# Self-attention in a transformer kernel: products of one or two units in 11 blocks, 11 key tiles summed by GpSimd, maxima negated in another form

## The chip, the cores and the metric

The kernel runs on one core of a Trainium2 chip. The metric is the time of one execution in device microseconds (us). Times inside the kernel are read from one profiled execution; its span starts at 0 and positions in it are given in us.

## The reference

Two transformer layers over x (2 x 2048 x 512), 16 heads of 32 channels each. The change lies in the only self-attention, that of the second layer, over all 2048 keys:

```python
scores = jnp.einsum('bqhd,bkhd->bhqk', qh, kh) / jnp.sqrt(jnp.asarray(d, q.dtype))
attn = jax.nn.softmax(scores, axis=-1)
out = jnp.einsum('bhqk,bkhd->bqhd', attn, vh)
```

Around it stand projections, a cross-attention over 77 context rows in each layer, normalizations and an MLP; they aren't touched.

## The kernel before

The function `attention` (L1592) works in 32 steps: 2 batches x 4 groups of 4 heads x 4 chunks of 512 queries. One step has 16 key tiles of 128 keys. Each engine has its own program with the same steps; semaphores join them. `run` (L1699) unrolls the first and last steps and loops over the rest.

**Two passes over the scores.** The softmax needs each query's largest score before the exponentials. So TensorE computes the scores twice. In the first form queries lie on the partitions: `score_unit` (L1785) is one matmul of 128 queries x 512 keys into one of three PSUM banks (`sm`), and VectorE's `peak_of_unit` (L1950) reduces it to its maxima. There are 64 units per step (4 heads x 4 query tiles x 4 key chunks). They run ahead: a step computes units 14 to 63 of the next step and 0 to 13 of the one behind that. A unit's matmul waits until the unit three before it has been reduced. When the last unit of a step is reduced (the 50th in the order of the running step, x = 49), `minus_peaks` (L1959) takes the maxima over the key chunks (`top`), negates them in two parts of lower precision (`neg_hi`, and the remainder) and lays them into `neg`; `turn_peaks` (L1801) transposes them on TensorE, ScalarE's `take_rows` (L1894) copies them out and a DMA spreads them into spare rows of `q`, so that the scores of the second pass come out with the maximum subtracted.

**The second pass.** `score_tile` (L1810): keys on the partitions, one matmul for each key tile and head, into one of three banks (`st`). ScalarE takes the exponential into `e` (`exponentials`, L1902), a ring of four tiles.

**The products.** `weigh` (L1822) multiplies a tile's exponentials by v for the four heads at once, each in its own 32 columns of the array, summed over the tiles in `acc[:, 0]`. `add_up` (L1837) does the same with a matrix of ones for the sums of the exponentials, in `acc[:, 1]`. To save such products, ten of the tiles (`POOLED`: 0, 1, 3, 4, 6, 7, 9, 10, 12, 13) are summed by GpSimd (`add`, L2021) into `esum`, which then needs one product. A unit of products is eight matmuls in the profile (four heads, each shown twice). A tile's place in the ring comes free when its products are done (`tile_used`) and, for a pooled tile, when GpSimd has added it (`e_added`).

**The order on TensorE** is written out in `step` (L1852). Behind each score matmul comes one unit of maxima. Behind the second head of every key tile comes a block of products (`weigh_tiles`): those of the tile before. A block has one unit for a pooled tile, two for another, three for the last, whose block holds `esum` as well: 16 blocks with 23 units.

```python
                        if NKT > 1 and h == 1:
                            if kt == 0 and exists(i, j - 1):
                                weigh_tiles(i, j - 1, [NKT - 1])
                            if kt > 0 and exists(i, j):
                                weigh_tiles(i, j, [kt - 1])
```

**The end of a step.** ScalarE copies `acc` to `sums` behind its exponentials of tile 0 of the next step (`fetch_sums`, L1921); only then may the next step's first product overwrite `acc`. VectorE transposes the sums of the exponentials, takes reciprocals, and transposes them back (`divide`, L1976) at the places `DIVIDE_AT` among its 64 reductions; GpSimd multiplies (`scale`, L2031) between its additions, and SyncE stores.

Of the kernel before, what the change touches and what calls it, by code (L numbers as in the profile page):

```python
# [7 lines left out]
F32 = mybir.dt.float32  # L8
F32R = mybir.dt.float32r
ALU = mybir.AluOpType  # L10
# [3 lines left out]
P = 128  # L14
B, T, C = 2, 2048, 512
S = 77
HEADS, DH = 16, 32
# [1574 lines left out]
def attention(nc, d, name, q_in, k_in, v_in, o_out, keys, preload):  # L1592
# [23 lines left out]

    POOLED = [t for t in range(NKT - 2) if t % 3 != 2] if NKT > 2 else []
    ADDS = max(len(POOLED) - 1, 0)
# [7 lines left out]
    LATE = 1 if NKT > 1 else 2  # L1626
    DIVIDE_AT = (6, 8, 32) if NKT > 1 else range(4)
    SETUP = 2 + KW % 2
    with nc.cleanup_on_exit(), ExitStack() as ctx:
# [15 lines left out]
        top = sb("top", [P, GH * TT])  # L1645
        neg_hi = sb("neg_hi", [P, GH * TT], F32R)
        neg = sb("neg", [P, TT, P])
        rows = sb("rows", [P, 2, W])
# [10 lines left out]
        unit_done, unit_read = sem("unit_done"), sem("unit_read")  # L1659
        top_done, neg_done, neg_ready = sem("top_done"), sem("neg_done"), sem("neg_ready")  # L1660
        score_done, score_read, tile_used, e_added = sem("score_done"), sem("score_read"), sem("tile_used"), sem("e_added")
# [6 lines left out]
        def exists(i, j):  # L1668

            return not isinstance(i, int) or 0 <= BODY * i + j < STEPS  # L1670
# [10 lines left out]
        def turned(i, j):  # L1681

            return number(i, j - 1, TURN) if j else 0
# [100 lines left out]
        def _(pe):  # L1784
# [16 lines left out]
            def turn_peaks(i, j):  # L1801

                pe.wait_ge(neg_ready, 2 * (BODY * i + j + 1))
                if j:
                    bank_free(pe, i, j - 1, TURN)
                for qt in range(TT):
                    mm = pe.transpose(st[:, TURN % RING if j else 0, qt * P:(qt + 1) * P], neg[:, qt], ident[:])
                mm.then_inc(score_done, 1)
# [28 lines left out]
            def add_up(i, j, kt):  # L1837

                if kt in POOLED:
                    return  # L1840
                first = min(t for t in range(NKT) if t not in POOLED)
                operands = [e[0:KR, (j * NKT + kt) % ER]]
                if POOLED and kt == NKT - 1:
                    pe.wait_ge(e_added, (BODY * i + j + 1) * ADDS)
                    operands.append(esum)
                for x, operand in enumerate(operands):
                    for h in range(GH):
                        mm = pe.matmul(acc[h * DH:(h + 1) * DH, 1], ones[0:KR], operand[:, h], start=(kt == first),  # L1848
                                       stop=(kt == NKT - 1 and x == len(operands) - 1), tile_position=(0, h * DH))
                mm.then_inc(tile_used, 1)  # L1850

            def step(i, j):  # L1852
                turn = exists(i, j + 1)
                units = units_of_step(i, j)
                given, scores = 0, 0
                if NKT == 1 and exists(i, j - 1):
                    weigh_tiles(i, j - 1, [0])
                for kt in range(NKT):
                    for h in range(GH):
                        if exists(i, j):  # L1860
                            score_tile(i, j, kt, h)
                        scores += 1
                        while given < len(units) and given * GH * NKT < scores * U:
                            score_unit(i, *units[given])
                            given += 1
                        if NKT > 1 and h == 1:
                            if kt == 0 and exists(i, j - 1):
                                weigh_tiles(i, j - 1, [NKT - 1])
                            if kt > 0 and exists(i, j):
                                weigh_tiles(i, j, [kt - 1])  # L1870
                    if kt == TURN_KT and turn:
                        turn_peaks(i, j + 1)
                for m, u in units[given:]:
                    score_unit(i, m, u)

            def weigh_tiles(i, j, tiles):

                for kt in tiles:
                    weigh(i, j, kt)
                    add_up(i, j, kt)  # L1880

# [11 lines left out]
        def _(act):  # L1893
# [33 lines left out]
            def step(i, j):  # L1927
                if NKT == 1 and exists(i, j - 1):
                    fetch_sums(i, j - 1)
                for kt in range(NKT):  # L1930
                    if exists(i, j):
                        exponentials(i, j, kt)
                    if NKT > 1 and kt == 4 and exists(i, j - 1):
                        spread_inverse(i, j - 1)
                    if NKT > 1 and kt == 0 and exists(i, j - 1):
                        fetch_sums(i, j - 1)
                    if kt == TURN_KT and exists(i, j + 1):
                        take_rows(i, j + 1)
# [10 lines left out]
        def _(dve):  # L1949
# [9 lines left out]
            def minus_peaks(i, j):  # L1959

                n = BODY * i + j
                dve.wait_ge(unit_read, (n + 1) * U + 2)
                if KC > 1:
                    dve.tensor_reduce(top[:], peak[:].rearrange("p (x c) -> p x c", c=KC), AX.X, ALU.max).then_inc(top_done, 1)
                    dve.wait_ge(top_done, n + 1)
                dve.tensor_scalar(neg_hi[:], top[:], -1.0, None, ALU.mult).then_inc(neg_done, 1)
                dve.wait_ge(neg_done, n + 1)
                if exists(i, j - 1):
                    dve.wait_ge(score_done, turned(i, j - 1) + 1)
                by_head = lambda ap: ap.rearrange("p (h t) -> p h t", t=TT)  # L1970
                parts = neg[:, :, 3 * DH:3 * DH + 2 * GH].rearrange("p t (h s) -> p h t s", s=2)
                dve.tensor_copy(parts[:, :, :, 0], by_head(neg_hi[:].bitcast(F32))).then_inc(neg_ready, 1)
                dve.scalar_tensor_tensor(out=parts[:, :, :, 1], in0=by_head(top[:]), scalar=-1.0, in1=by_head(neg_hi[:].bitcast(F32)),
                                         op0=ALU.mult, op1=ALU.subtract).then_inc(neg_ready, 1)
# [33 lines left out]
            dve.memset(ones[:], 1.0).then_inc(set_up, 1)  # L2008
            dve.memset(neg[:], 0.0).then_inc(set_up, 1)
            if KE > KW:  # L2010
# [9 lines left out]
        def _(pool):  # L2020
# [16 lines left out]
            def step(i, j):  # L2037
                if POOLED and exists(i, j):
                    for x in range(1, 6):
                        add(i, j, x)  # L2040
                if exists(i, j - LATE):
                    scale(i, j - LATE)
                if POOLED and exists(i, j):
                    for x in range(6, len(POOLED)):
                        add(i, j, x)
# [245 lines left out]
```

## Time and profile before

| | us |
|---|---|
| median of 3 runs | 4163.22 (4161.48 to 4164.41) |
| profiled execution | 4159.49 |
| its span | 4157.7 |
| TensorE busy, whole span | 3771.6 |
| VectorE | 2333.9 |
| ScalarE | 1867.3 |
| GpSimd | 2080.2 |
| self-attention, first unit to last copy of the sums | 905.6 to 2804.0 |

In the profile PE is TensorE's matmuls, PEld its weight loads (one in front of each matmul, and the place where it waits), DVE is VectorE, ACT ScalarE, POOL GpSimd. `a_` stands before the names of this function's tiles: `a_sm` and `a_st` are the scores of the two passes, `a_e` the exponentials, `a_peak` the maxima, `a_acc` the products. A row gives start, length, engine, line, operation, tiles and the count of instructions that it joins; in square brackets the idle time before it and what ended it. Lengths of matmuls are modelled; starts of weight loads are the better measure of TensorE's pace.

### The profile page before, as it was taken

How to read it: one execution, taken by the hardware profiler on the slowest of the kernel's cores; microseconds unless marked ns; L12 is line 12 of the kernel's file. 1: busy time of each engine (PE TensorE's matmuls, PEld its weight loads, DVE VectorE, ACT ScalarE, POOL GpSimd, SP SyncE). 2: the span in 40 equal slices, each digit the busy share in tenths (PEclk: the TensorE clock that was granted, in tenths of full speed). 3: DMA queues.
4: the chain of work that ended last, by engine and by line, in shares of the span. 5: the costliest groups of instructions: out<-in, count | busy, mean ns of one | idle time of the engine just before them, and what ended most of it. 6: DMA issues, size and time to landing. Idle time of an engine off the chain costs nothing. (4 is left out here: it accounts for less than half of the span.)

```text
span 4157.7 us, 58861 instructions
## 1 busy us (share of the span) xinstructions
PE 3771.6 (91%) x19596; PEld 2442.6 (59%) x19596; DVE 2333.9 (56%) x4020; ACT 1867.3 (45%) x3431; POOL 2080.2 (50%) x923
## 2 busy tenths in 40 slices
PE   4799969979999999999999999985999959999998
PEld 2577748854444444444444444433777737888887
DVE  2466642247777767776777777733676625222222
ACT  1465631115666656665666666663565521111111
POOL 0356630005778767776777777783676634000000
PEclk8788879978999999999999999997999869999999
DMA  7566657752130211203130211105567651211110
GB/s 230 133 158 173 168 154 220 227 137 62 26 67 16 64 27 38 46 23 67 26 67 15 65 26 26 31 18 134 135 165 173 164 166 56 81 40 40 40 40 30
DMA packets 213560, 371.98 MB, mean 89 GB/s; under 512 B 36103, under 2 KB 52999, under 8 KB 209703
## 3 DMA queue, kind: packets, MB, share of 16 engines
q1 hardware_dynamic: 213287, 368.49, 32.7%
q8 instruction: 153, 2.51, 0.3%
q14 instruction: 120, 0.98, 0.1%
HBM read 215.54 MB, written 144.51 MB: 87 GB/s over the span
## 5 line engine op out<-in xcount | busy, mean ns | idle before, releaser
L1957 DVE TENSOR_REDUCE a_peak<-a_sm 128x1 f32<-128x512 f32 x2048 | 1275.0, 682 | 470.5 <-PE a_sm L1797 464.5
L1911 ACT ACTIVATE a_e<-a_st 128x512 f32<-128x512 f32 x2048 | 1075.1, 600 | 718.2 <-PE a_st L1819 714.7
L2029 POOL TENSOR_TENSOR a_esum<-a_esum,a_e 128x2048 f32<-128x2048 f32 x256 | 1172.1, 4578 | 126.5 <-ACT a_e L1911 114.1
L1819 PE MATMUL a_st<-a_q,a_k 128*128 128x512 f32 x2048 | 870.2, 428 | 17.9 <-issue 12.9
L1797 PE MATMUL a_sm<-a_k,a_q 96*128 96x512 f32 x2048 | 831.8, 413 | 49.7 <-DMA a_k<-s_k 28.1
L1819 PEld LDWEIGHTS a_st<-a_q,a_k 128*128 128x128 f32 x2048 | 386.4, 189 | 536.7 <-ACT a_e L1911 269.9
L1832 PE MATMUL a_acc<-a_e,a_v 128*32 128x512 f32 x4096 | 547.2, 606 | 17.6 <-ACT a_sums L1925 16.7
L1797 PEld LDWEIGHTS a_sm<-a_k,a_q 96*128 96x128 f32 x2048 | 397.8, 194 | 148.8 <-DVE a_peak L1957 57.6
L2152 PE MATMUL mlp_ph<-mlp_us,mlp_w_hi 128*128 128x512 f32 x1024 | 336.3, 391 | 31.9 <-DVE mlp_raw_lo L2201 31.9
L2029 POOL TENSOR_TENSOR a_esum<-a_e 128x2048 f32<-128x2048 f32 x32 | 146.8, 4587 | 427.6 <-ACT a_e L1911 427.6
L2194 ACT ACTIVATE mlp_gelu<-mlp_ph,mlp_b 128x512 f32<-128x512 f32 x128 | 88.1, 688 | 595.4 <-PE mlp_ph L2152 595.4
L2209 DVE CAST mlp_gs<-mlp_gelu 128x512 fp32r<-128x512 f32 x128 | 91.4, 714 | 458.3 <-ACT mlp_gelu L2194 458.3
L2167 PE MATMUL mlp_py<-mlp_w_hi,mlp_gs 128*128 128x512 f32 x1024 | 317.7, 391 | 17.1 <-DVE mlp_gs L2211 17.1
L2232 POOL TENSOR_TENSOR mlp_x<-mlp_x,mlp_brow 128x2048 f32<-128x2048 f32 x8 | 37.0, 4626 | 569.5 <-DMA mlp_x<-s_x 569.3
L1409 POOL TENSOR_TENSOR p_e<-p_e,p_inv 128x308 f32<-128x308 f32 x256 | 173.4, 709 | 168.6 <-DVE p_inv L1093 168.6
L2152 PEld LDWEIGHTS mlp_ph<-mlp_us,mlp_w_hi 128*128 128x128 f32 x1024 | 193.2, 189 | 72.6 <-issue 32.3
L2167 PEld LDWEIGHTS mlp_py<-mlp_w_hi,mlp_gs 128*128 128x128 f32 x1024 | 192.0, 188 | 61.6 <-issue 16.5
L587 PE MATMUL p_sm<-p_ks,p_qs 96*128 96x78 f32 x1024 | 171.9, 310 | 47.7 <-DMA p_qs<-s_q 28.3
L587 PEld LDWEIGHTS p_sm<-p_ks,p_qs 96*128 96x128 f32 x1024 | 157.2, 222 | 80.9 <-issue 28.9
L1848 PE MATMUL a_acc<-a_e,a_ones 128*32 128x512 f32 x1536 | 201.4, 596 | 1.7 <-POOL a_esum L2029 1.7
L2167 PE MATMUL mlp_py<-mlp_raw_lo,mlp_gs 128*128 128x512 f32 x512 | 200.0, 391 | 0.0
L2152 PE MATMUL mlp_ph<-mlp_us,mlp_raw_lo 128*128 128x512 f32 x512 | 199.9, 390 | 0.0
(151 smaller groups left out, 5169.7 us busy)
## 6 DMA issues: line engine op xcount, KB each, us to landing
p_qs<-s_q SPq DMA_DIRECT2D x192, 256.0 KB, 5.7
s_q<-p_qo SPq DMA_DIRECT2D x64, 512.0 KB, 7.4
a_q<-s_q SPq DMA_DIRECT2D x96, 256.0 KB, 5.2
a_k<-s_k SPq DMA_DIRECT2D x24, 1024.0 KB, 15.5
s_x<-p_x SPq DMA_DIRECT2D x16, 1024.0 KB, 4.4
s_u<-p_ut_hi SPq DMA_DIRECT2D x64, 256.0 KB, 5.8
s_u<-p_ut_lo SPq DMA_DIRECT2D x64, 256.0 KB, 6.4
p_us<-s_u SPq DMA_DIRECT2D x16, 1024.0 KB, 7.8
```

The costliest lines, as they stand in the source:

```text
L587: mm = pe.matmul(sm[:, unit % 2, h * KE:(h + 1) * KE], qs[0:3 * DH, g % 2, h, qt * P:(qt + 1) * P], ks[0:3 * DH, b, g * GH + h], start=Tru ...
L1409: pool.tensor_tensor(e[:, number % 2, qt, :, 0:S], e[:, number % 2, qt, :, 0:S], inv[:, number % 2, qt].unsqueeze(2).to_broadcast([P, GH, ...
L1797: mm = pe.matmul(sm[:, bank_of_unit(j, u), x * KE:(x + 1) * KE], q[0:3 * DH, j % QR, h, qt * P:(qt + 1) * P], k[0:3 * DH, g % 2, h, kc * K ...
L1819: pe.matmul(st[0:KR, place(kt, h) % RING], k[:, g % 2, h, kt * P:kt * P + KR], q[:, j % QR, h], start=True, stop=True).then_inc(score_done, 1)
L1832: mm = pe.matmul(acc[rows, 0], v[0:KR, g % 2, kt, rows], e[0:KR, (j * NKT + kt) % ER, h], start=(kt == 0), stop=(kt == NKT - 1), tile_posi ...
L1848: mm = pe.matmul(acc[h * DH:(h + 1) * DH, 1], ones[0:KR], operand[:, h], start=(kt == first), stop=(kt == NKT - 1 and x == len(operands) - ...
L1911: act.activation(e[0:KR, (j * NKT + kt) % ER, h], st[0:KR, place(kt, h) % RING], ACT.Exp, scale=SCALE).then_inc(score_read, 1)
L1957: dve.tensor_reduce(dst, src, AX.X, ALU.max).then_inc(unit_read, 1)
L2029: pool.tensor_tensor(esum[:], e[:, slot(0)] if x == 1 else esum[:], e[:, slot(x)], ALU.add).then_inc(e_added, 1)
L2152: mm = pe.matmul(ph[:, m % 4], w1[pw][:, t, m * P:(m + 1) * P], us[:, b, pm, t], start=(t == 0 and s == 0), stop=(t == KT - 1 and s == 2))
L2167: mm = pe.matmul(py[:, tt], gs[:, m % 2, pw, tt * P:(tt + 1) * P], w2[pm][:, m], start=(m == 0 and s == 0), stop=(m == HT - 1 and s == 2))
L2209: dve.tensor_copy(gs[:, m % 2, 0], gelu[:, m % 2]).then_inc(g_hi, 1)
```

## The change

`POOLED` becomes 0, 1, 2, 4, 5, 7, 8, 10, 11, 12, 13: eleven tiles are summed by GpSimd in ten additions. A new function `products` writes the order of the blocks out: eleven blocks of two units, behind the second head of tiles 0, 1, 2, 4, 5, 7, 8, 10, 11, 13 and 15. The product of `esum` has a function of its own. The copy of `acc`, the places of the divisions and of GpSimd's scaling move to fit. `minus_peaks` has no tensor_scalar and no copy any more: two operations of two tensors and a scalar write the parts into `neg` directly, the first with a tensor of zeros.

```diff
-    POOLED = [t for t in range(NKT - 2) if t % 3 != 2] if NKT > 2 else []
+    POOLED = [0, 1, 2, 4, 5, 7, 8, 10, 11, 12, 13]
...
-    DIVIDE_AT = (6, 8, 32) if NKT > 1 else range(4)
+    DIVIDE_AT = (10, 12, 36)
...
-        neg_hi = sb("neg_hi", [P, GH * TT], F32R)
-        neg = sb("neg", [P, TT, P])
+        zeros = sb("zeros", [P, TT])
+        neg = sb("neg", [P, TT, P], F32R)
...
             def add_up(i, j, kt):
...
+                for h in range(GH):
+                    mm = pe.matmul(acc[h * DH:(h + 1) * DH, 1], ones[0:KR], e[0:KR, (j * NKT + kt) % ER, h], start=(kt == first),
+                                   stop=False, tile_position=(0, h * DH))
+                if kt < NKT - 1:
+                    mm.then_inc(tile_used, 1)
+
+            def add_partial(i, j):
+
+                pe.wait_ge(e_added, (BODY * i + j + 1) * ADDS)
+                for h in range(GH):
+                    mm = pe.matmul(acc[h * DH:(h + 1) * DH, 1], ones[0:KR], esum[:, h], start=False, stop=True, tile_position=(0, h * DH))
                 mm.then_inc(tile_used, 1)
+
+            def products(i, j, kt):
+
+                if kt == 0 and exists(i, j - 1):
+                    add_up(i, j - 1, 14)
+                    weigh(i, j - 1, 15)
+                elif kt == 1 and exists(i, j - 1):
+                    add_up(i, j - 1, 15)
+                    add_partial(i, j - 1)
+                elif kt == 2 and exists(i, j):
+                    weigh(i, j, 0)
+                    weigh(i, j, 1)
+                elif kt == 4 and exists(i, j):
+                    weigh(i, j, 2)
+                    weigh(i, j, 3)
+                elif kt == 5 and exists(i, j):
+                    add_up(i, j, 3)
+                    weigh(i, j, 4)
...
+                elif kt == 15 and exists(i, j):
+                    weigh(i, j, 13)
+                    weigh(i, j, 14)
...
-                        if NKT > 1 and h == 1:
-                            if kt == 0 and exists(i, j - 1):
-                                weigh_tiles(i, j - 1, [NKT - 1])
-                            if kt > 0 and exists(i, j):
-                                weigh_tiles(i, j, [kt - 1])
+                        if h == 1:
+                            products(i, j, kt)
...
-                    if NKT > 1 and kt == 0 and exists(i, j - 1):
+                    if kt == 1 and exists(i, j - 1):
                         fetch_sums(i, j - 1)
...
-                dve.tensor_scalar(neg_hi[:], top[:], -1.0, None, ALU.mult).then_inc(neg_done, 1)
-                dve.wait_ge(neg_done, n + 1)
...
-                dve.tensor_copy(parts[:, :, :, 0], by_head(neg_hi[:].bitcast(F32))).then_inc(neg_ready, 1)
-                dve.scalar_tensor_tensor(out=parts[:, :, :, 1], in0=by_head(top[:]), scalar=-1.0, in1=by_head(neg_hi[:].bitcast(F32)),
+                no_term = zeros[:].unsqueeze(1).to_broadcast([P, GH, TT])
+                dve.scalar_tensor_tensor(out=parts[:, :, :, 0], in0=by_head(top[:]), scalar=-1.0, in1=no_term, op0=ALU.mult,
+                                         op1=ALU.add).then_inc(neg_ready, 1)
+                dve.wait_ge(neg_ready, 2 * n + 1)
+                dve.scalar_tensor_tensor(out=parts[:, :, :, 1].bitcast(F32), in0=by_head(top[:]), scalar=-1.0, in1=parts[:, :, :, 0].bitcast(F32),
                                          op0=ALU.mult, op1=ALU.subtract).then_inc(neg_ready, 1)
...
                 if POOLED and exists(i, j):
-                    for x in range(1, 6):
+                    for x in range(1, 8):
                         add(i, j, x)
                 if exists(i, j - LATE):
                     scale(i, j - LATE)
                 if POOLED and exists(i, j):
-                    for x in range(6, len(POOLED)):
+                    for x in range(8, len(POOLED)):
                         add(i, j, x)
```

## Rows read from the trace of the kernel before

**Rows 1.** Busy time by engine in one step's length, with the granted clock.

```profile
2000.00:2057.40 57.40, 56.13 (x318) 27.58 (x317) 43.30 (x72) 35.30 (x68) 42.41 (x11) 1.00 0.10 24
```

The columns are: stretch, its length; busy us and instructions of PE, PEld, DVE, ACT, POOL; granted clock; share of the DMA engines; GB/s.

**Rows 2.** Instructions in order of time, ScalarE: copies of the sums.

```profile
1417.19 1.03 ACT L1925 ACTIVATE a_sums<-a_acc 128x1024 f32<-128x1024 f32 x1
...
1541.22 1.03 ACT L1925 ACTIVATE a_sums<-a_acc 128x1024 f32<-128x1024 f32 x1
...
1598.62 1.03 ACT L1925 ACTIVATE a_sums<-a_acc 128x1024 f32<-128x1024 f32 x1
```

**Rows 3.** In order of time, TensorE's weight loads around two ordinary blocks.

```profile
1506.09 0.19 PEld L1819 LDWEIGHTS a_st<-a_q,a_k 128*128 128x128 f32 x1 [0.84 <-ACT a_e L1911]
1506.20 0.19 PEld L1797 LDWEIGHTS a_sm<-a_k,a_q 96*128 96x128 f32 x1
...
1507.61 0.19 PEld L1797 LDWEIGHTS a_sm<-a_k,a_q 96*128 96x128 f32 x1
1508.15 0.16 PEld L1832 LDWEIGHTS a_acc<-a_e,a_v 128*32 128x32 f32 x8 [0.36 <-issue]
1509.15 0.19 PEld L1819 LDWEIGHTS a_st<-a_q,a_k 128*128 128x128 f32 x1 [0.84 <-ACT a_e L1911]
...
1511.22 0.16 PEld L1832 LDWEIGHTS a_acc<-a_e,a_v 128*32 128x32 f32 x8 [0.36 <-issue]
...
1513.08 0.19 PEld L1819 LDWEIGHTS a_st<-a_q,a_k 128*128 128x128 f32 x1 [0.84 <-issue]
```

**Rows 4.** The same view, the stretch in which the maxima are negated.

```profile
1523.13 0.19 PEld L1819 LDWEIGHTS a_st<-a_q,a_k 128*128 128x128 f32 x1 [0.84 <-issue]
...
1525.78 0.19 PEld L1797 LDWEIGHTS a_sm<-a_k,a_q 96*128 96x128 f32 x1 [1.17 <-DVE a_peak L1957]
1526.21 0.16 PEld L1832 LDWEIGHTS a_acc<-a_e,a_v 128*32 128x32 f32 x8 [0.24 <-issue]
```

**Rows 5.** In order of time, VectorE.

```profile
1506.86 1.89 DVE L1957 TENSOR_REDUCE a_peak<-a_sm 128x1 f32<-128x512 f32 x3 [0.58 <-PE a_sm L1797]
...
1519.98 2.48 DVE L1957 TENSOR_REDUCE a_peak<-a_sm 128x1 f32<-128x512 f32 x4 [0.58 <-PE a_sm L1797]
...
1522.75 1.75 DVE L1966 TENSOR_SCALAR a_neg_hi<-a_top 128x16 fp32r<-128x16 f32 x1
...
1525.03 2.49 DVE L1957 TENSOR_REDUCE a_peak<-a_sm 128x1 f32<-128x512 f32 x4
...
1544.14 0.69 DVE L1957 TENSOR_REDUCE a_peak<-a_sm 128x1 f32<-128x512 f32 x1 [1.17 <-PE a_sm L1797]
...
1546.70 1.82 DVE L1957 TENSOR_REDUCE a_peak<-a_sm 128x1 f32<-128x512 f32 x3
```

**Rows 6.** In order of time, GpSimd: two additions, the scaling, two additions.

```profile
1504.81 9.23 POOL L2029 TENSOR_TENSOR a_esum<-a_esum,a_e 128x2048 f32<-128x2048 f32 x2 [0.74 <-ACT a_e L1911]
1514.00 1.29 POOL L2035 TENSOR_TENSOR a_o<-a_sums,a_inv_t 128x512 f32<-128x512 f32 x1
1515.25 9.23 POOL L2029 TENSOR_TENSOR a_esum<-a_esum,a_e 128x2048 f32<-128x2048 f32 x2
```

**Rows 7.** VectorE beside GpSimd elsewhere; shortest/median/longest of such operations (ns).

```profile
150.23 1.27 POOL L1403 TENSOR_TENSOR p_us_lo<-p_us,p_us_hi 128x512 fp32r<-128x512 f32 x1
...
150.85 2.80 DVE L1161 SCALAR_TENSOR_TENSOR raw_p_lo<-raw_p,p_w 128x2048 fp32r<-128x2048 f32 x1
...
L1161 DVE SCALAR_TENSOR_TENSOR raw_p_lo<-raw_p,p_w x6: 2281/2288/2798, 96.5 to 3042.7; 128x2048 fp32r<-128x2048 f32 x6
...
3450.45 4.93 POOL L2225 TENSOR_TENSOR mlp_raw_lo<-mlp_raw,mlp_w_hi 128x2048 fp32r<-128x2048 f32 x1
3450.84 4.82 DVE L2209 CAST mlp_gs<-mlp_gelu 128x512 fp32r<-128x512 f32 x1
...
L2209 DVE CAST mlp_gs<-mlp_gelu x128: 418/427/4824, 3433.4 to 4142.3; 128x512 fp32r<-128x512 f32 x128
```

**Rows 8.** Weight loads in order of time: the first one behind a halt.

```profile
1475.77 0.29 PEld L1819 LDWEIGHTS a_st<-a_q,a_k 128*128 128x128 f32 x1 [6.88 <-issue]
```

More of the change, by code:

```diff
@@ L1626, in attention @@
     LATE = 1 if NKT > 1 else 2
-    DIVIDE_AT = (6, 8, 32) if NKT > 1 else range(4)
-    SETUP = 2 + KW % 2
+    DIVIDE_AT = (10, 12, 36)
+    SETUP = 3 + KW % 2
     with nc.cleanup_on_exit(), ExitStack() as ctx:
@@ L1659, in attention @@
         unit_done, unit_read = sem("unit_done"), sem("unit_read")
-        top_done, neg_done, neg_ready = sem("top_done"), sem("neg_done"), sem("neg_ready")
+        top_done, neg_ready = sem("top_done"), sem("neg_ready")
         score_done, score_read, tile_used, e_added = sem("score_done"), sem("score_read"), sem("tile_used"), sem("e_added")
@@ L1806, in turn_peaks @@
                 for qt in range(TT):
-                    mm = pe.transpose(st[:, TURN % RING if j else 0, qt * P:(qt + 1) * P], neg[:, qt], ident[:])
+                    mm = pe.transpose(st[:, TURN % RING if j else 0, qt * P:(qt + 1) * P], neg[:, qt].bitcast(F32), ident[:])
                 mm.then_inc(score_done, 1)
@@ L1837, in add_up @@
             def add_up(i, j, kt):
-                if kt in POOLED:
-                    return
                 first = min(t for t in range(NKT) if t not in POOLED)
[L1842 to L1849, printed above, removed]
@@ new lines, in products @@
+            def products(i, j, kt):
[14 more added lines that the diff above has]
+                    weigh(i, j, 4)
+                elif kt == 7 and exists(i, j):
+                    weigh(i, j, 5)
+                    weigh(i, j, 6)
+                elif kt == 8 and exists(i, j):
+                    add_up(i, j, 6)
+                    weigh(i, j, 7)
+                elif kt == 10 and exists(i, j):
+                    weigh(i, j, 8)
+                    weigh(i, j, 9)
+                elif kt == 11 and exists(i, j):
+                    add_up(i, j, 9)
+                    weigh(i, j, 10)
+                elif kt == 13 and exists(i, j):
+                    weigh(i, j, 11)
+                    weigh(i, j, 12)
+                elif kt == 15 and exists(i, j):
+                    weigh(i, j, 13)
+                    weigh(i, j, 14)
@@ L1855, in step @@
                 given, scores = 0, 0
-                if NKT == 1 and exists(i, j - 1):
-                    weigh_tiles(i, j - 1, [0])
                 for kt in range(NKT):
@@ L1874, in step @@
                     score_unit(i, m, u)
[L1876 to L1880, printed above, removed]
             pe.sem_inc(tile_used, ER)
@@ L1927, in step @@
             def step(i, j):
-                if NKT == 1 and exists(i, j - 1):
-                    fetch_sums(i, j - 1)
                 for kt in range(NKT):
@@ L1932, in step @@
                         exponentials(i, j, kt)
-                    if NKT > 1 and kt == 4 and exists(i, j - 1):
+                    if kt == 4 and exists(i, j - 1):
                         spread_inverse(i, j - 1)
-                    if NKT > 1 and kt == 0 and exists(i, j - 1):
+                    if kt == 1 and exists(i, j - 1):
                         fetch_sums(i, j - 1)
@@ L1965, in minus_peaks @@
                     dve.wait_ge(top_done, n + 1)
-                dve.tensor_scalar(neg_hi[:], top[:], -1.0, None, ALU.mult).then_inc(neg_done, 1)
-                dve.wait_ge(neg_done, n + 1)
                 if exists(i, j - 1):
                     dve.wait_ge(score_done, turned(i, j - 1) + 1)
+                parts = neg[:, :, 3 * DH:3 * DH + 2 * GH].rearrange("p t (h s) -> p h t s", s=2)
                 by_head = lambda ap: ap.rearrange("p (h t) -> p h t", t=TT)
-                parts = neg[:, :, 3 * DH:3 * DH + 2 * GH].rearrange("p t (h s) -> p h t s", s=2)
-                dve.tensor_copy(parts[:, :, :, 0], by_head(neg_hi[:].bitcast(F32))).then_inc(neg_ready, 1)
-                dve.scalar_tensor_tensor(out=parts[:, :, :, 1], in0=by_head(top[:]), scalar=-1.0, in1=by_head(neg_hi[:].bitcast(F32)),
+                no_term = zeros[:].unsqueeze(1).to_broadcast([P, GH, TT])
[3 more added lines that the diff above has]
+                dve.scalar_tensor_tensor(out=parts[:, :, :, 1].bitcast(F32), in0=by_head(top[:]), scalar=-1.0, in1=parts[:, :, :, 0].bitcast(F32),
                                          op0=ALU.mult, op1=ALU.subtract).then_inc(neg_ready, 1)
@@ L2008, in _ @@
             dve.memset(ones[:], 1.0).then_inc(set_up, 1)
-            dve.memset(neg[:], 0.0).then_inc(set_up, 1)
+            dve.memset(neg[:].bitcast(F32), 0.0).then_inc(set_up, 1)
+            dve.memset(zeros[:], 0.0).then_inc(set_up, 1)
             if KE > KW:
```

## The prediction

> **What bounds the kernel now.** I read the busy shares by window first. In one step of the attention TensorE is busy 56.13 of 57.40 us at full clock, VectorE 43.30, ScalarE 35.30, GpSimd 42.41 [rows 1]. The three others have room on average, so a gain must come from TensorE's stream, and a loss from a moment at which one of the others makes TensorE wait. The steps are even: the copies of the sums, one per step, lie 57.40 us apart (1541.22, 1598.62) [rows 2]. There are 32 steps.
>
> Then the weight loads in order of time, since they show when TensorE issues. Call a score matmul with the maxima matmul behind it a slot. Between two blocks of products stand four slots. They take 2.06 us (1506.09 to 1508.15), the maxima loads inside 0.47 apart (1506.20 to 1507.61, three pitches). A block of one unit (the eight matmuls of one tile) takes 1.00, one of two 1.86 [rows 3]. So a further unit costs 0.86, and a block as such costs 1.00 - 0.86 = 0.14 plus 2.06 - 4 x 0.47 = 0.18 in the slots around it: 0.32.
>
> **What the change takes out of TensorE's stream.** One tile of ones products goes (11 tiles summed by GpSimd, not 10): 0.86. The blocks go from 16 to 11: 5 x 0.32 = 1.60. Together 2.46 us per step. Third, the wait at the maxima: behind unit 49 of a step VectorE negates them. The tensor_scalar took 1.75 us from 1522.75 while a GpSimd addition was running (the second of the pair from 1515.25, until 1524.48), and the next reduction began at 1525.03 [rows 5, 6]; the stretch of four slots took 3.08 (1523.13 to 1526.21), 1.02 too long [rows 4]. At most 3.48 is thus to be had.
>
> **What it puts in.** Products now stand behind key tiles 0, 1, 2, 4, 5, 7, 8, 10, 11, 13, 15, none behind 3, 6, 9, 12, 14. So five stretches have eight slots. A maxima matmul needs one of three banks: its load waits for the reduction three units earlier. Reductions start 0.77 behind the stretch's start (1506.86), run at 0.60 ((2.48 - 0.69) / 3) and last 0.69 [rows 5]; the released load comes 0.06 behind the end (1525.03 + 0.69 = 1525.72 against 1525.78) [rows 4, 5]. In four slots only the last load depends on a reduction of its own stretch: 0.77 + 0.69 + 0.06 = 1.52, which is exactly when it comes (1507.61). In eight slots the last load would come at 1.52 + 4 x 0.47 = 3.40 and may come at 0.77 + 4 x 0.60 + 0.75 = 3.92: 0.52 late. The block follows a waiting load sooner (0.43 against 0.54, 1525.78 to 1526.21 and 1507.61 to 1508.15) [rows 3, 4]: 0.41 lost per bare stretch of eight. TensorE's blocks then give VectorE time to catch up.
> - Slots 10 to 17 hold the transpose behind unit 10 and the reciprocal behind unit 12. Now they stretch three reductions from 1.80 to 2.56 us (1544.14 to 1546.70) [rows 5]: 0.41 + 0.76 = 1.17. Before, they stood behind the first unit of a stretch of four and cost nothing.
> - Slots 22 to 29: 0.41.
> - Slots 34 to 41, second transpose behind unit 36: the larger part of those 0.76, taken as 0.62: 1.03.
> - Slots 46 to 53: minus the peaks, behind unit 49.
> - Slots 54 to 61: the four transposes of the maxima give VectorE 0.45; ScalarE's copy of the rows stands in the way instead. I take 0.2, between 0 and 0.5.
>
> For slots 46 to 53 the small operations without any waiting take about 0.85: 2.77 - 2.40 = 0.37 up to the first negation (1519.98 to 1522.75, less four reductions), and 0.55 from the lock's end (1524.48) to the next reduction, less the copy that goes [rows 5, 6]. 0.41 + 0.85 = 1.26. Whether they wait is the question of this case. They are two operations of two SBUF tensors instead of a tensor_scalar, a copy and one such. The only row of this form that meets GpSimd is in an earlier stage: a scalar_tensor_tensor takes 2.29 alone, but 2.80 where it began at 150.85 with a GpSimd operation running to 151.50 [rows 7]. So it waits for GpSimd. And the two take turns: in the MLP a subtraction of GpSimd, queued behind a VectorE operation, got in between it and VectorE's next cast, which then took 4.82 us, 0.43 being usual [rows 7].
>
> The Trainium skill, VectorE: DVE Perf Modes, section Mode 2x_2P, reserves the two-port mode for operations of one source; by that rule alone the new operations would be free, and the sum would be the first rival's below. The same skill, SBUF — State Buffer, section Who interferes with whom, says that two SBUF inputs contend with a GpSimd operation that reads SBUF. The row above decides for the second.
>
> What does GpSimd do at that moment? Let the four slots 42 to 45 start at 0. Tile 10 is complete and its addition starts at 1.79 (1504.81, against the stretch at 1506.09 - 1.00 - 2.07 = 1503.02), GpSimd being idle: its previous additions ended over 1 us before. An addition takes its place for 4.6 (two from 1504.81 to the scaling at 1514.00), the scaling for 1.25 (to 1515.25) [rows 6]. So: scaling at 6.39, the next addition (tile 11, long complete) at 7.64, the one behind it at 12.3. VectorE: the stretch 46 to 53 starts at 2.07 + 1.86 = 3.93; reductions from 4.70; the first negation is wanted 2.77 later (1519.98 to 1522.75) [rows 5], at 7.47. That is inside the scaling's last 0.2 us. It gets in at 7.6, in front of the addition; the addition takes its turn, and the second negation waits for its whole 4.6 us, to 12.35. The next reduction starts at 12.5, ends at 13.2, and the last load comes at 13.25, 9.32 after the stretch's start, where 3.40 was natural: 5.9 - 0.1 = 5.8 us lost.
>
> Sum per step: -2.46 - 1.02 + 1.17 + 0.41 + 1.03 + 5.8 + 0.2 = **+5.1 us**. Of the 32 steps 30 have all their units and one most: 30.5 x 5.1 = 156.
>
> **The clock.** Twice TensorE halted for 6.88 us, and the granted clock was at the lower level when it resumed: the load at 1475.77 took 0.29, not 0.19 [rows 8, 3]. The two intervals from 1417.19 to 1541.22 [rows 2] were 9.2 longer than twice 57.40, 2.3 beyond the halt; waits of 1 us left the clock alone. The halt here is 5.8, nearer to the 6.88. Bounds 0 and 2.3; I take 1.5, as some would escape: 46 us.
>
> **Edits that cost little.** GpSimd's tenth addition: 32 x 4.6 = 147 us of its time lie beside TensorE's 62 us step (47 busy); the additions of tiles 12 and 13 end before their slots are wanted, by 1 us or more. Without that cover each would delay ScalarE. In the last step, where no maxima are left, GpSimd is nearly the bound, and one more addition shows: 0 to 4.6, I take 3, less 1 for the blocks: +2. The copy of the sums moves one tile later together with the first product it frees; its wait stays. One more memset: under 0.1.
>
> Against the profiled execution's 4159.5: 4159.5 + 156 + 46 + 2 = 4364; the median of the runs is 3.7 higher: **4368 us**.
>
> **The rivals.**
> 1. No lock for these operations, the stalls as worked out: 1.26 in place of 5.8, so +0.6 per step, no clock loss: 4163 + 18 + 2 = 4183. For it: the old scalar_tensor_tensor is short wherever it stands, and so small an operation of this form never met a running addition; against it: the row at 150.85.
> 2. Both negations miss their turn. If the first comes 0.2 us later or GpSimd is earlier, it waits for the addition of tile 11 and the second for that of tile 12: 4.6 more per step, clock loss always: 4163 + 30.5 x (9.7 + 2.3) + 2 = 4531. The margin is 0.2 us, but the distances in it repeat from step to step, so it is less likely.
> 3. Faster. The lock does not hold and the reductions keep up in stretches of eight, so that only the extras are paid: 4 x 0.41 less than rival 1, -1.0 per step: 4133. It decides from 0.15 us less per stretch of eight. For it: VectorE is busy only 43 of 57 us; against it: its last load in four slots already comes without slack.
>
> A milder form of the forecast (the second negation waits for the scaling alone) gives some 4195.
>
> **How the numbers follow.** The forecast has 0.55, rival 1 0.17, rival 2 0.10, rival 3 0.13, the milder form 0.05. About 0.2% (8 us) is what a measurement of this kernel can tell from no change. Slower: 0.55 + 0.10 + 0.05 and 0.12 of rival 1, 0.82; the same 0.05; faster 0.13. The forecast's own range is 4305 (no clock loss) to 4400. To leave out no more than 2 in 10 the range must reach down over the milder form and rival 1 into the nearer part of rival 3, 4140, and up to 4410.
>
> **What would show each step.** Weight loads: stretches of eight with a wait for a_peak before the last maxima loads, about 0.4 per bare one; two-unit blocks of 1.86; eleven per step. The first negation at most 0.3 us, the second about 4.6, GpSimd additions on both sides. A step interval of 62.5 to 64.5 us. Ones products on e tiles 1280, not 1536; additions 320, not 288. It is wrong if both negations take 0.18 with an addition running (rival 1), or if stretches of eight take 3.94 (rival 3).

## The result, and the profile of the changed kernel

| | before | after |
|---|---|---|
| median (4 runs of each, side by side) | 4162.35 us | 4374.9 us (4366.89 to 4376.5) |
| profiled execution, its span | 4159.49, 4157.7 | 4366.89, 4365.1 |
| TensorE, VectorE busy | 3771.6, 2333.9 | 3822.5, 2403.3 |
| ScalarE, GpSimd busy | 1867.3, 2080.2 | 1874.5, 2224.0 |

The ratio of the times is 1.0508 [1.0493, 1.0523]: slower by 5.1%. The forecast was 4368 us.

Where the time went is seen first in the copies of the sums, as in [rows 2]. In order of time, ScalarE, after:

```profile
1544.64 1.03 ACT L1951 ACTIVATE a_sums<-a_acc 128x1024 f32<-128x1024 f32 x1
1608.51 1.03 ACT L1951 ACTIVATE a_sums<-a_acc 128x1024 f32<-128x1024 f32 x1
...
1866.89 1.03 ACT L1951 ACTIVATE a_sums<-a_acc 128x1024 f32<-128x1024 f32 x1
1931.68 1.03 ACT L1951 ACTIVATE a_sums<-a_acc 128x1024 f32<-128x1024 f32 x1
```

A step now takes 64.79 us (1931.68 - 1866.89), 63.87 in the one before 1608.51, where it took 57.40. From the first copy to the last the stage is 209.5 us longer (1020.46 to 3017.64, against 1015.30 to 2802.96). The spans differ by 207.4. So everything happens in this stage.

Within a step, the weight loads of slots 46 to 53, the counterpart of [rows 4]:

```profile
1579.22 0.19 PEld L1819 LDWEIGHTS a_st<-a_q,a_k 128*128 128x128 f32 x1 [0.84 <-issue]
...
1588.50 0.29 PEld L1797 LDWEIGHTS a_sm<-a_k,a_q 96*128 96x128 f32 x1 [5.66 <-DVE a_peak L1981]
1589.22 0.20 PEld L1832 LDWEIGHTS a_acc<-a_e,a_v 128*32 128x32 f32 x8 [0.43 <-issue]
...
1592.43 0.19 PEld L1819 LDWEIGHTS a_st<-a_q,a_k 128*128 128x128 f32 x1 [1.30 <-issue]
```

The last maxima load of the stretch waits 5.66 us for a reduction, so eight slots take 10.00 us (1579.22 to 1589.22), and the block of two units behind them takes 3.21 instead of 1.86; the row of its first loads lasts 0.20 where it was 0.16. VectorE and GpSimd at that moment, for [rows 5, 6]:

```profile
1580.00 2.48 DVE L1981 TENSOR_REDUCE a_peak<-a_sm 128x1 f32<-128x512 f32 x4 [1.44 <-PE a_sm L1797]
1582.52 0.22 DVE L1988 TENSOR_REDUCE a_top<-a_peak 128x16 f32<-128x64 f32 x1
1582.88 4.52 DVE L1995 SCALAR_TENSOR_TENSOR a_neg<-a_top,a_zeros 128x16 fp32r<-128x16 f32 x1
1587.44 0.19 DVE L1998 SCALAR_TENSOR_TENSOR a_neg<-a_top,a_neg 128x16 f32<-128x16 f32 x1
1587.75 2.48 DVE L1981 TENSOR_REDUCE a_peak<-a_sm 128x1 f32<-128x512 f32 x4
```

```profile
1581.62 1.28 POOL L2061 TENSOR_TENSOR a_o<-a_sums,a_inv_t 128x512 f32<-128x512 f32 x1
1582.87 9.14 POOL L2055 TENSOR_TENSOR a_esum<-a_esum,a_e 128x2048 f32<-128x2048 f32 x2
```

One of the two negations waits for a whole addition of GpSimd, 4.52 us for an operation of 0.19. It is the first, which asks 0.01 us behind the addition's start, and not the second. All 32 steps by tile, shortest, median and longest in ns (the first two steps of the stage, at 943 and 995 us, aren't like the others: 0.19 and 3.53):

```profile
L1995 DVE SCALAR_TENSOR_TENSOR a_neg<-a_top,a_zeros x32: 186/4529/4585, 943.0 to 2946.0; 128x16 fp32r<-128x16 f32 x32
L1998 DVE SCALAR_TENSOR_TENSOR a_neg<-a_top,a_neg x32: 187/189/190, 943.2 to 2950.7; 128x16 f32<-128x16 f32 x32
```

Windows behind the same wait, with the columns of [rows 1]: the granted clock is 0.50 there, the lower level of 1.2 GHz, and 1.00 from 1593.00 on. In a step like most others, whose wait ends at 1910.78, it is still 0.50 at 1914 to 1916 (last line):

```profile
1588.50:1591.50 3.00, 3.00 (x13) 0.88 (x17) 1.74 (x3) 0.00 (x0) 3.00 (x1) 0.50 0.00 0
...
1593.00:1640.00 47.00, 45.75 (x255) 22.17 (x254) 33.36 (x56) 29.51 (x56) 32.02 (x7) 1.00 0.13 29
...
1914.00:1916.00 2.00, 2.00 (x10) 0.82 (x3) 0.00 (x0) 0.09 (x1) 0.28 (x1) 0.50 0.00 0
```

The maxima loads in the costliest groups of the page, after. The wait for the maxima is 351.1 us in all; it was 57.6 before. Not all of that is loss: it is 221.4 in the first experiment below, which is as fast as the kernel before.

```profile
L1797 PEld LDWEIGHTS a_sm<-a_k,a_q 96*128 96x128 f32 x2048 | 404.4, 198 | 424.5 <-DVE a_peak L1981 351.1
```

### The profile page after: what moved, and what is told of

The parts are those of the page before. It is cut to its first block and busy times, and to the rows that moved or that the text cites. A ratio compares the mean times of both kernels' runs of the same rounds, so it can differ in the third digit from the quotient of the medians.

```text
span 4365.1 us, 58478 instructions
## 1 busy us (share of the span) xinstructions
PE 3822.5 (88%) x19340; PEld 2432.1 (56%) x19340; DVE 2403.3 (55%) x3989; ACT 1874.5 (43%) x3431; POOL 2224.0 (51%) x955
## 5 line engine op out<-in xcount | busy, mean ns | idle before, releaser
L2055 POOL TENSOR_TENSOR a_esum<-a_esum,a_e 128x2048 f32<-128x2048 f32 x288 | 1315.5, 4568 | 239.4 <-ACT a_e L1937 226.6
L1797 PE MATMUL a_sm<-a_k,a_q 96*128 96x512 f32 x2048 | 884.4, 439 | 206.2 <-DVE a_peak L1981 178.2
L1797 PEld LDWEIGHTS a_sm<-a_k,a_q 96*128 96x128 f32 x2048 | 404.4, 198 | 424.5 <-DVE a_peak L1981 351.1
L1832 PE MATMUL a_acc<-a_e,a_v 128*32 128x512 f32 x4096 | 558.2, 652 | 18.0 <-ACT a_sums L1951 15.8
L1832 PEld LDWEIGHTS a_acc<-a_e,a_v 128*32 128x32 f32 x4096 | 119.8, 115 | 296.9 <-issue 202.0
```

The costliest lines, as they stand in the source:

```text
L1797: mm = pe.matmul(sm[:, bank_of_unit(j, u), x * KE:(x + 1) * KE], q[0:3 * DH, j % QR, h, qt * P:(qt + 1) * P], k[0:3 * DH, g % 2, h, kc * K ...
L1832: mm = pe.matmul(acc[rows, 0], v[0:KR, g % 2, kt, rows], e[0:KR, (j * NKT + kt) % ER, h], start=(kt == 0), stop=(kt == NKT - 1), tile_posi ...
L2055: pool.tensor_tensor(esum[:], e[:, slot(0)] if x == 1 else esum[:], e[:, slot(x)], ALU.add).then_inc(e_added, 1)
```

## The experiments

Each ratio is to the kernel before as it was timed beside them: 4156.2 us for the first four experiments, 4156.81 for the last three.

**No addition behind the scaling.** The changed kernel, in which the additions of tiles 11, 12 and 13 are left out, so the sums of the exponentials lack these tiles:

```diff
+                if x >= 8:
+                    pool.sem_inc(e_added, 1)
+                    return
                 pool.tensor_tensor(esum[:], e[:, slot(0)] if x == 1 else esum[:], e[:, slot(x)], ALU.add).then_inc(e_added, 1)
```

> The changed kernel without GpSimd's additions behind its scaling (those of tiles 11, 12 and 13 are left out, so the sums of the exponentials lack them; waits and counts are kept). Theory (the first negation waits for the addition that starts behind the scaling): it waits for nothing longer than the rest of the scaling, 0.2 us; the stretch of slots 46 to 53 takes 5.2 instead of 10.0, the clock stays at its upper level, a step takes 57.9 instead of 64.8 us: 4375 - 30.5 x 6.9 = 4165. Rival (the two operations are slow by themselves, or TensorE waits for something else there): the step stays at 64 to 65, 4375.

Measured: 4157.11 us (4150.74 to 4161.85), ratio to before 1.0004 [0.9994, 1.0014]. Its negations by tile, then VectorE in order of time:

```profile
L1995 DVE SCALAR_TENSOR_TENSOR a_neg<-a_top,a_zeros x32: 185/186/190, 941.7 to 2740.6; 128x16 fp32r<-128x16 f32 x32
```

```profile
1578.08 0.19 DVE L1995 SCALAR_TENSOR_TENSOR a_neg<-a_top,a_zeros 128x16 fp32r<-128x16 f32 x1
1578.31 0.19 DVE L1998 SCALAR_TENSOR_TENSOR a_neg<-a_top,a_neg 128x16 f32<-128x16 f32 x1
1578.62 2.48 DVE L1981 TENSOR_REDUCE a_peak<-a_sm 128x1 f32<-128x512 f32 x4
```

Neither waits any more. Slots 46 to 53 on TensorE, and one window of a step's length:

```profile
1574.44 0.19 PEld L1819 LDWEIGHTS a_st<-a_q,a_k 128*128 128x128 f32 x1 [0.84 <-issue]
...
1579.37 0.19 PEld L1797 LDWEIGHTS a_sm<-a_k,a_q 96*128 96x128 f32 x1 [1.31 <-DVE a_peak L1981]
1579.79 0.16 PEld L1832 LDWEIGHTS a_acc<-a_e,a_v 128*32 128x32 f32 x8 [0.24 <-issue]
```

```profile
2000.00:2057.85 57.85, 55.71 (x309) 26.99 (x308) 41.33 (x71) 35.40 (x68) 33.28 (x8) 1.00 0.10 24
```

The stretch takes 5.35 us instead of 10.00, the clock stays at 1.00, and the usual interval of the copies is 57.81 to 57.87. So the whole loss hangs on the meeting with the addition: 64.79 - 57.85 = 6.94 us per step. The other stretches of eight are the same with and without these additions (5.04, 4.34 and 4.94), so it isn't GpSimd's total work. Of the 6.94, 4.65 are the wait (10.00 - 5.35) and the other 2.3 the clock: in an ordinary step the block behind the wait takes 3.57 instead of 1.85, and slots 54 to 61 take 5.12 instead of 4.58. In the step of 63.87 the clock took 1.4 (6.02 - 4.65), nearly all of it in the one block (3.21 - 1.86 = 1.35). The second finding: the new order of the blocks doesn't win even without the wait. It stays 0.45 us per step above before's 57.40: it takes out 3.48 (2.46 + 1.02), so by the difference the stretches of eight put back 3.93. The total is no slower than before all the same, because the last step has three additions fewer to wait for (its interval is 45.53, before 50.60) and the two steps with a halt, before's 66.62 and 66.16, are 63.56 and 63.54.

**The old form of the negation in the changed kernel.** Everything else of the change stays:

```diff
-                dve.scalar_tensor_tensor(out=parts[:, :, :, 0], in0=by_head(top[:]), scalar=-1.0, in1=no_term, op0=ALU.mult,
-                                         op1=ALU.add).then_inc(neg_ready, 1)
+                dve.tensor_scalar(neg_hi[:], top[:], -1.0, None, ALU.mult).then_inc(neg_done, 1)
+                dve.wait_ge(neg_done, n + 1)
...
+                dve.tensor_copy(parts[:, :, :, 0], by_head(neg_hi[:].bitcast(F32))).then_inc(neg_ready, 1)
```

> The changed kernel with the negation of before (tensor_scalar, copy, one operation of two tensors). Theory (where it stands beside GpSimd's work decides, not its form): the tensor_scalar is wanted 0.03 us behind the maxima instead of 0.14, inside the scaling; it or the copy behind it waits for the whole next addition, 4.5 us either way; step 64.5 to 65, 4375 plus or minus 10. Rival (the new form is to blame): each waits as before for 1.8 us at most, step about 60, 4230.

Measured: 4374.67 us (4368.55 to 4377.2), ratio 1.0529 [1.0512, 1.0547]. By tile:

```profile
L1990 DVE TENSOR_SCALAR a_neg_hi<-a_top x32: 174/177/4581, 947.5 to 2950.6; 128x16 fp32r<-128x16 f32 x32
...
L1996 DVE COPY a_neg<-a_neg_hi x32: 180/4331/4349, 947.7 to 2955.2; 128x16 f32<-128x16 f32 x32
```

Now the tensor_scalar gets in and the copy waits a whole addition, in 24 of the steps; in the last six it is the tensor_scalar that waits (4.53 to 4.58) and the copy that gets in. The time is that of the changed kernel. The form of the operations is indifferent: one with a single source waits as one with two does.

**The new form in the kernel before**, and nothing else (the same lines the other way round):

> The kernel before with the new negation alone. Theory: the first operation is wanted at the old place, 1.6 us before an addition ends, waits 1.6 us for it, and one operation less follows: TensorE's stretch is 2.9 instead of 3.08, step 57.2, 4155. Rival (the form of two tensors doesn't wait for GpSimd): both take 0.2 us, the stretch is 2.07, step 56.4, 4131.

Measured: 4150.14 us (4148.44 to 4157.5), ratio 0.9995 [0.9985, 1.0004]; no difference that this measurement can tell, though the interval of the copies is 57.20 us, as expected, against 57.40. By tile:

```profile
L1971 DVE SCALAR_TENSOR_TENSOR a_neg<-a_top,a_zeros x32: 186/1691/1849, 938.9 to 2725.3; 128x16 fp32r<-128x16 f32 x32
L1974 DVE SCALAR_TENSOR_TENSOR a_neg<-a_top,a_neg x32: 187/189/191, 939.1 to 2727.2; 128x16 f32<-128x16 f32 x32
```

The first negation waits as the tensor_scalar of [rows 5] did, and the second doesn't. Here that says nothing about turns: no addition was queued. The next one waits for ScalarE's exponentials and starts only behind the second negation. VectorE and GpSimd in one step:

```profile
1515.78 0.19 DVE L1974 SCALAR_TENSOR_TENSOR a_neg<-a_top,a_neg 128x16 f32<-128x16 f32 x1
```

```profile
1516.13 9.22 POOL L2031 TENSOR_TENSOR a_esum<-a_esum,a_e 128x2048 f32<-128x2048 f32 x2 [0.43 <-ACT a_e L1911]
```

The kernel before has the same gap, 0.44 us at 1524.91. What both show is only that either form waits for an addition that is running.

**Eleven tiles on GpSimd in the old blocks.** One product of ones fewer per step, the scaling one addition later, the old negation:

```diff
-    POOLED = [t for t in range(NKT - 2) if t % 3 != 2] if NKT > 2 else []
+    POOLED = [0, 1, 2, 3, 4, 6, 7, 9, 10, 12, 13]
...
-                    for x in range(1, 6):
+                    for x in range(1, 7):
...
```

> The kernel before (16 blocks, old negation) with 11 tiles for GpSimd: 0, 1, 2, 3, 4, 6, 7, 9, 10, 12, 13, the scaling one addition later. TensorE has 0.86 us less per step. Theory (GpSimd's phase at the negation decides): the early additions run without a gap and push the one of tile 10 until 3.3 us behind the wish for the negation, so TensorE loses 1.5 us more than before, or 6 if the copy behind it waits for the next addition as well: step 58 to 63, 4180 to 4330. Rival (only TensorE's work counts): step 56.5, 4136.

Measured: 4355.81 us (4353.17 to 4363.46), ratio 1.0487 [1.0469, 1.0504]. TensorE has less to do, and the kernel is 4.9% slower, more than the 4180 to 4330 expected. VectorE, then GpSimd, in order of time:

```profile
2036.83 0.22 DVE L1964 TENSOR_REDUCE a_top<-a_peak 128x16 f32<-128x64 f32 x1
2037.09 4.25 DVE L1966 TENSOR_SCALAR a_neg_hi<-a_top 128x16 fp32r<-128x16 f32 x1
2041.47 4.45 DVE L1972 COPY a_neg<-a_neg_hi 128x16 f32<-128x16 f32 x1
2045.83 0.17 DVE L1973 SCALAR_TENSOR_TENSOR a_neg<-a_top,a_neg_hi 128x16 f32<-128x16 f32 x1
```

```profile
2030.84 1.28 POOL L2035 TENSOR_TENSOR a_o<-a_sums,a_inv_t 128x512 f32<-128x512 f32 x1
2032.09 13.79 POOL L2029 TENSOR_TENSOR a_esum<-a_esum,a_e 128x2048 f32<-128x2048 f32 x3
```

Three additions run back to back over the negation, and two of its operations miss: 8.7 us. In a step of 64.9 us the stretch of four slots takes 10.10 instead of 3.08, and the block behind it 1.87 instead of 1.00, at a granted clock of 0.50. (In the last six steps the copy follows the tensor_scalar by 0.03 us instead of 0.13 and gets in; the interval of the copies falls from 64.9 to between 60.6 and 61.8.) This is the second rival's picture in another kernel. It needs no new blocks and no new form, only a GpSimd that is busy when the maxima are negated.

**The wait for the transposes ahead of the reduction of the maxima.** In the changed kernel the first negation is wanted later than `a_top` allows: 1582.88 against 1582.52 + 0.22, 0.14 behind it, where the old tensor_scalar follows 0.04 behind (2036.83 + 0.22 to 2037.09 in eleven_only); the wait for `score_done` now stands between them. (In the first two and the last six steps of the changed kernel it is 0.03.) My theory was that with this wait out of the way both would get in. The rival was the prediction's: the first gets in at the scaling's end, the second waits.

```diff
                 n = BODY * i + j
+                if exists(i, j - 1):
+                    dve.wait_ge(score_done, turned(i, j - 1) + 1)
                 dve.wait_ge(unit_read, (n + 1) * U + 2)
...
-                if exists(i, j - 1):
-                    dve.wait_ge(score_done, turned(i, j - 1) + 1)
```

> The changed kernel with one wait moved: VectorE waits for the transposes of the step before ahead of the maxima's reduction, no longer between it and the first negation. Theory (a race at the scaling's end, lost by under 0.1 us): the negation is wanted 0.1 us sooner, gets in at the scaling's end, the second follows within 0.05 us and gets in too; no wait over 0.3, step 57.9 instead of 64.8, 4165. Rival (turns are taken, as the prediction had it: the second then waits for the whole next addition): the first 0.2, the second 4.5, step 64.7, 4370.

Measured: 4370.99 us (4365.21 to 4374.91), ratio 1.0519 [1.0504, 1.0533]. VectorE, then GpSimd:

```profile
1577.55 0.22 DVE L1990 TENSOR_REDUCE a_top<-a_peak 128x16 f32<-128x64 f32 x1
1577.81 0.19 DVE L1995 SCALAR_TENSOR_TENSOR a_neg<-a_top,a_zeros 128x16 fp32r<-128x16 f32 x1
1578.03 4.42 DVE L1998 SCALAR_TENSOR_TENSOR a_neg<-a_top,a_neg 128x16 f32<-128x16 f32 x1
```

```profile
1576.66 1.28 POOL L2061 TENSOR_TENSOR a_o<-a_sums,a_inv_t 128x512 f32<-128x512 f32 x1
1577.90 9.09 POOL L2055 TENSOR_TENSOR a_esum<-a_esum,a_e 128x2048 f32<-128x2048 f32 x2
```

My theory fell. In 24 steps the first negation gets in, in the scaling's last moments, and the second finds the addition running and waits for it. In the last six it is the other way round: the first asks 0.04 to 0.07 us behind the addition's start, waits 4.5 us, and the second gets in. The forecast had described this kernel's 24 steps, not the changed one; the cost is the same, one addition.

**The divisions in stretches of four**, on top of the last kernel:

```diff
-    DIVIDE_AT = (10, 12, 36)
+    DIVIDE_AT = (18, 19, 42)
...
-                    if kt == 4 and exists(i, j - 1):
+                    if kt == 5 and exists(i, j - 1):
```

> The same, with VectorE's divisions behind units 18, 19 and 42, all in stretches of four slots, and ScalarE's spreading of the inverse one tile later. Theory (an operation of VectorE costs TensorE its full length in a stretch of eight and nothing early in a stretch of four): slots 10 to 17 and 34 to 41 take 4.34 as the bare ones do, instead of 5.03 and 4.94; step 1.3 less than in the run with the wait ahead, 56.6 if that has 57.9; 40 us less in all. Rival (it is VectorE's total work that counts): no difference to that run.

Measured: 4321.95 us (4317.75 to 4324.06), ratio 1.0396 [1.0381, 1.041]; 49 us less than the kernel it was built on. Weight loads of slots 10 to 17, here and in the changed kernel:

```profile
1599.47 0.19 PEld L1819 LDWEIGHTS a_st<-a_q,a_k 128*128 128x128 f32 x1 [0.84 <-issue]
...
1603.82 0.16 PEld L1832 LDWEIGHTS a_acc<-a_e,a_v 128*32 128x32 f32 x8 [0.25 <-ACT a_e L1937]
```

```profile
1547.58 0.19 PEld L1819 LDWEIGHTS a_st<-a_q,a_k 128*128 128x128 f32 x1 [0.84 <-issue]
...
1552.61 0.16 PEld L1832 LDWEIGHTS a_acc<-a_e,a_v 128*32 128x32 f32 x8 [0.24 <-issue]
```

4.35 against 5.03 us. The transpose (0.70) and the reciprocal (0.23) cost most of their length in a stretch of eight and nothing in one of four: 0.68 here and 0.59 in slots 34 to 41 (a transpose of 0.70), 1.27 per step or 39 us in 30.5. The steps are now 62.5 to 63.7 long (the copies at 1659.94, 1722.47 and 1786.15), alternately. The gain beyond 39 us is the clock's: in the shorter steps it comes back sooner. The block behind the wait and slots 54 to 61 take 7.98 us there (from 1703.03, mean granted clock 0.80) and 8.92 in the longer ones (from 1765.75, clock 0.70), as in the ordinary steps of wait_ahead (8.85 to 8.97).

**Sixteen blocks, eleven tiles, and a GpSimd whose additions end in time.** From the findings: keep the old blocks with their stretches of four, take the one product of ones away, put the scaling behind the sixth addition, choose tiles 0, 1, 2, 4, 5, 6, 8, 9, 10, 12, 13, and use the new negation with the wait ahead:

```diff
-    POOLED = [t for t in range(NKT - 2) if t % 3 != 2] if NKT > 2 else []
+    POOLED = [0, 1, 2, 4, 5, 6, 8, 9, 10, 12, 13]
...
-                    for x in range(1, 6):
+                    for x in range(1, 7):
...
```

> The kernel before with its 16 blocks in stretches of four, 11 tiles for GpSimd (0, 1, 2, 4, 5, 6, 8, 9, 10, 12, 13), its scaling behind the addition of tile 8, the new negation and its wait ahead. Theory (stretches of four let VectorE keep up; GpSimd's addition of tile 9 ends 0.2 us behind the wish for the negation): TensorE has 0.86 less per step, and of the 1.02 at the maxima 0.8 or more goes; step 55.6 to 55.9, faster than before by 45 to 55 us. Rival (the phase is missed, the negation waits for the addition of tile 10): step 59 to 62, slower than before by 60 to 140 us.

Measured: 4118.4 us (4113.87 to 4125.68), ratio 0.9908 [0.9892, 0.9924]: 0.9% faster than the kernel before. VectorE, GpSimd and the weight loads:

```profile
1562.52 0.35 DVE L1971 SCALAR_TENSOR_TENSOR a_neg<-a_top,a_zeros 128x16 fp32r<-128x16 f32 x1
1562.90 0.19 DVE L1974 SCALAR_TENSOR_TENSOR a_neg<-a_top,a_neg 128x16 f32<-128x16 f32 x1
1563.67 2.48 DVE L1957 TENSOR_REDUCE a_peak<-a_sm 128x1 f32<-128x512 f32 x4 [0.58 <-PE a_sm L1797]
```

```profile
1558.23 18.65 POOL L2031 TENSOR_TENSOR a_esum<-a_esum,a_e 128x2048 f32<-128x2048 f32 x4
```

```profile
1562.90 0.19 PEld L1819 LDWEIGHTS a_st<-a_q,a_k 128*128 128x128 f32 x1 [0.84 <-issue]
...
1564.96 0.16 PEld L1832 LDWEIGHTS a_acc<-a_e,a_v 128*32 128x32 f32 x8 [0.36 <-issue]
```

Four additions run back to back over the negation, but the first of them ends just behind the moment at which the first negation asks (1558.23 + 18.65 / 4 = 1562.89, against 1562.52). So the first negation takes 0.35, and the second gets in behind it. VectorE's next reduction waits for TensorE, not the other way round, and the stretch has its natural 2.06. Before, it took 3.08 [rows 4]. A step takes 55.84 (1809.67 to 1865.51 between copies), 1.56 less than before: 1.02 from the wait and most of the rest, 0.50, from the product (0.86, less 0.36 by which the block of three units grew, 3.07 instead of 2.71, since it now waits for GpSimd's last addition). This is luck of position as much as design. In one step of the 32 the second negation, 0.03 us behind the first as in the others, asked 0.01 us behind the next addition's start and waited for all of it:

```profile
1674.69 4.57 DVE L1974 SCALAR_TENSOR_TENSOR a_neg<-a_top,a_neg 128x16 f32<-128x16 f32 x1
```

The interval of the copies is 61.90 us there. This and the last two intervals (55.94 and 53.78 us, before 54.86 and 50.60) are why the kernel is 38 us faster and not the 45 to 55 expected.

## Why the prediction was right, and where it was not

The size came out well: 4368 against 4374.9 us, and a step of 62.5 to 64.5 forecast against 63.6 to 65.0, most of them 64.8. That one whole addition is waited for was right; which operation waits was not, and that the total still fits is partly luck. Point by point:

| term, us | forecast | measured |
|---|---|---|
| block of two units | 1.86 | 1.85 to 1.86 |
| bare stretch of eight (22 to 29) | 3.94 + 0.41 = 4.35 | 4.34 |
| slots 10 to 17 | 5.11 | 5.03 |
| slots 34 to 41 | 4.97 | 4.94 |
| slots 46 to 53 | 9.7 | 10.00 |
| the same without a lock (rival 1) | 5.2 | 5.35 |
| step without a lock (rival 1) | 57.40 + 0.6 = 58.0 | 57.85 |
| clock per step | 1.5, between 0 and 2.3 | 1.4 to 2.3 |
| tail | +2 | +0.1 on the last interval (50.67 against 50.60) |

- **TensorE's stream** held to 0.1 us in every stretch but that of the wait (0.3). The rule behind it (reductions at 0.60 against slots at 0.47, three banks) carries: divide_in_fours shows the same price from the other side.
- **The collision** was right in kind and in size. GpSimd's queue stood where it was worked out to stand: with slots 42 to 45 starting at 1575.31, the scaling came at 6.31 (1581.62) and the next addition at 7.56 (1582.87); 6.39 and 7.64 were forecast. The first negation was wanted at 7.57, and 7.47 was forecast.
- **The step that failed** is "It gets in at 7.6, in front of the addition; the addition takes its turn, and the second negation waits". In the changed kernel the first waited, in all 30 full steps (4.52 to 4.58), and the second took 0.19. Two things were wrong. The first negation was put where the old tensor_scalar had been, right behind `a_top`; but the change moved the `score_done` wait in front of it, 0.1 us, and the margin was 0.2. Without that 0.1 it got in, in 24 steps of wait_ahead. The 0.1 isn't all, though: in the last six steps of the changed kernel the negation follows `a_top` by 0.03, asks 0.03 us ahead of the addition's start (2621.86 against 2621.89) and waits too; there the maxima end 0.06 later against GpSimd's scaling. And "take turns" is no rule: behind a whole addition a second small operation got in as well (changed kernel, sixteen_blocks). Had the first error stood alone, with turns taken, it would have been rival 2 and 4531 us. The two errors cancelled: wait_ahead, which has the first right, waits at the second, and its ratio is the same (1.0519 against 1.0508).
- **The clock** was undersized. "Some would escape" didn't happen: the ordinary steps lose 2.3, the upper bound, and only those behind a halt less (1.4 in the first). For the stage 204 us were forecast and 209.5 came, and this close a match is luck: an ordinary step is 7.4 us longer than before where 6.6 (5.1 + 1.5) were forecast, but four of the 31 intervals between copies, the two with a halt in them and the last two, are only 3.8, 4.7, 4.2 and 0.1 longer.
- **The forecast's own range** starts at 4305 "(no clock loss)"; 4368 less the 46 us of the clock is 4322. Nothing else rests on it.
- **Rival 1** was the right number for another kernel, the one without additions there. Its reason, that such operations take no lock, is refuted by the 4.52 of the changed kernel. What the prediction took from the Trainium skill, SBUF — State Buffer, section Who interferes with whom, agrees with the trace: an operation with two SBUF inputs was blocked for the whole of GpSimd's instruction (4.52 us). The other rule weighed there, of the Trainium skill, VectorE: DVE Perf Modes, section Mode 2x_2P, keeps the two-port mode for one source; that the copy, of one source, is blocked as well in old_negation (4.33 us) doesn't contradict it. The case turned on something else: on who is next when an operation of GpSimd ends.
- **Rival 3** asked stretches of eight at 3.94; they were 4.34. Fallen.
- **GpSimd's extra addition** was costed at nothing in itself. That holds outside the collision: without the late additions the other stretches are as long as with them. At the one place where VectorE asks, an addition of 4.6 us costs 6.9 per step, wait and clock together.

What stays open: what decides the race within the few hundredths of a microsecond in which both engines ask. Whether an earlier place of the negation, in GpSimd's idle time, would be better still wasn't tried.

## What to carry to other kernels

Average load says little about an engine that shares something with another. GpSimd had 15 us free in each step; what counted was whether one addition runs at the one moment at which a 0.2 us operation stands between TensorE and its next bank. When a change adds work to GpSimd, lay its queue and VectorE's critical operations on one time axis, with the waits in front of each, and treat a margin of 0.2 us as none. And before fewer, larger blocks are taken for a gain, look whether the smaller ones gave another engine the time to catch up: five stretches of eight cost more here (0.4 each, and most of the length of each VectorE operation in them) than five blocks fewer gave back (0.32 each).

## What the runs showed of the hardware that was not expected

- A waiting VectorE operation gets in between two GpSimd operations that are queued back to back, and whether the next one does as well depends on when it asks, against the recorded start of the next addition. I counted the first two operations of each negation that asked within 0.45 us of the start of a queued addition, in the six kernels that have such meetings. All 139 that asked 0.06 us or more ahead of it got in before it. All 138 that asked 0.04 us or more behind it waited for the rest of the addition, 4.2 us or more; among them are the second negations of wait_ahead, 0.03 us behind the first (4.42 us), and the copies of eleven_only, 0.13 behind the tensor_scalar (4.45 us). In between, from 0.03 ahead to 0.02 behind, all 36 that asked at the end of a scaling (128x512) waited, and 47 of 48 that asked at the end of an addition (128x2048) got in. Records of GpSimd are rough at this scale, and why the two differ isn't shown.
- A wait of 5.66 us for TensorE in a step of 64.8 brought the granted clock to 0.50 for three to five microseconds behind it, and cost a third to a half of its own excess again (1.4 to 2.3 beside 4.65).
- Operations of 128x16 elements with one source (tensor_scalar, copy) and with two (scalar_tensor_tensor) waited alike for GpSimd: 4.25, 4.33 and 4.52 us, against 0.17 to 0.19 undisturbed.
